# Routing inside the attention, and a second block at its end: a single-core attention and mixture-of-experts kernel

## The reference

```
x1  = layernorm(x + attention(x))                      # x: (8, 1024, 256)
gates = softmax(x1 @ gate_w);  topw, topi = top_k(gates, 2);  topw /= sum(topw)
h   = gelu(layernorm(x1 @ w1[e] + b1[e]) * ln1_g[e] + ln1_b[e])   # 256 -> 512
y_e = h @ w2[e] + b2[e]                                           # 512 -> 256
out = layernorm(layernorm(x1 + sum_k topw_k * y_topi_k) * ln_g + ln_b + x1)
```

## Time and profile before

| | us |
|---|---|
| median of 3 runs | 2865.77 (2865.7 to 2875.63) |
| profiled execution, whole | 2861.65 |
| profiled execution, span of the core | 2859.9 |
| attention's last copy of its output ends | 1800.2 |
| attention's block ends, routing begins | 1840.3 |
| routing ends, experts begin | 2070.0 |
| experts end, combine begins | 2624.6 |

### The profile page before, as it was taken

One profiled execution on the slowest core, in us unless ns is written; L12 is line 12 of the kernel. 1 busy time (PEld: TensorE's weight loads), 2 busy tenths in 40 slices (PEclk: granted clock), 3 DMA queues, 4 the chain that ended last, 5 costly groups with the idle time before them and its releaser, 6 DMA issues. The chain is left out here.

```text
span 2859.9 us, 40717 instructions
## 1 busy us (share of the span) xinstructions
PE 2070.0 (72%) x11695; PEld 1411.8 (49%) x11696; DVE 1752.2 (61%) x4841; ACT 1329.2 (46%) x3188; POOL 1324.5 (46%) x1487
## 2 busy tenths in 40 slices
PE   2588888888888888889889889400099999996000
PEld 2444554554554554555555554200088888885000
DVE  2466575576576576576576574241067777775998
ACT  0154544554555555555555556111067777775112
POOL 1354444354354354454454352157644444443885
PEclk7698998998998998998997998655599999998555
DMA  3767667667567567567667663243022222222453
GB/s 112 107 119 127 100 104 140 97 104 143 96 105 143 96 104 145 98 104 143 98 104 143 97 103 75 47 57 46 4 64 68 68 68 68 68 68 89 145 169 110
DMA packets 189312, 282.09 MB, mean 99 GB/s; under 512 B 52236, under 2 KB 110356, under 8 KB 189100
## 3 DMA queue, kind: packets, MB, share of 16 engines
q1 hardware_dynamic: 172332, 244.79, 45.7%
q0 software_dynamic: 16768, 34.69, 4.3%
HBM read 97.53 MB, written 37.62 MB: 47 GB/s over the span
## 5 line engine op out<-in xcount | busy, mean ns | idle before, releaser
L488 ACT ACTIVATE probs<-scores_T 128x512 f32<-128x512 f32 (+3 forms) x1536 | 660.0, 492 | 426.6 <-PE scores_T L387 424.2
L650 POOL TENSOR_SCALAR_AFFINE_SELECT probs<-probs 128x256 f32<-128x256 f32 x512 | 205.2, 409 | 855.7 <-ACT probs L488 854.9
L445 PE MATMUL ring<-k_stack,q_stack_b 96*128 96x512 f32 (+3 forms) x1024 | 408.0, 445 | 43.5 <-DVE neg_part L577 34.9
L577 DVE TENSOR_REDUCE neg_part<-ring 128x1 f32<-128x512 f32 x512 | 330.9, 680 | 104.5 <-PE ring L445 102.1
L582 DVE CUSTOM_DVE_ANT_0 ring<-ring,mask 128x384 f32<-128x384 f32 (+3 forms) x512 | 240.5, 515 | 243.5 <-PE ring L445 241.4
L387 PE MATMUL scores_T<-q_stack_b,k_stack 98*128 98x512 f32 (+3 forms) x1024 | 336.3, 408 | 34.0 <-ACT probs L488 33.3
L404 PE MATMUL o_ps<-probs,v_ones 128*17 128x512 f32 (+3 forms) x3072 | 357.0, 539 | 0.1
L445 PEld LDWEIGHTS ring<-k_stack,q_stack_b 96*128 96x128 f32 x1024 | 198.4, 205 | 264.5 <-DVE neg_part L577 94.6
L582 DVE CUSTOM_DVE_ANT_0 ring<-ring,mask,neg_part 128x384 f32<-128x384 f32 (+3 forms) x512 | 259.9, 554 | 68.7 <-PE ring L445 67.8
L993 ACT ACTIVATE g<-ht_ps,ln_b,ln_g 128x128 f32<-128x128 f32 x544 | 217.6, 450 | 135.6 <-PE ht_ps L943 135.6
L387 PEld LDWEIGHTS scores_T<-q_stack_b,k_stack 98*128 98x128 f32 x1024 | 200.7, 212 | 92.6 <-ACT probs L488 67.0
(11 more groups left out here) (176 smaller groups left out, 4497.9 us busy)
## 6 DMA issues: line engine op xcount, KB each, us to landing
u_rot<-u SPq DMA_DIRECT2D x128, 256.0 KB, 3.7
k_stack<-u_rot SPq DMA_DIRECT2D x128, 256.0 KB, 6.6
y_rows<-y_out SPq DMA_DIRECT2D x136, 128.0 KB, 2.1
lat_w<-lat_split SPq DMA_DIRECT2D x32, 512.0 KB, 8.1
q_stack_a<-u_rot SPq DMA_DIRECT2D x64, 256.0 KB, 7.6
q_stack_b<-u_rot SPq DMA_DIRECT2D x64, 256.0 KB, 10.3
k_stack<-u SPq DMA_DIRECT2D x64, 256.0 KB, 6.2
x_raw<-in_xT SPq DMA_DIRECT2D x16, 512.0 KB, 5.1
```

Of the source, the lines that this page charges most:

```text
L445: nc.tensor.matmul(out[:, 0:k1 - k0], q_stack[qb // 4][0:3 * L, row_buf(n, qb // 4), h, P * (qb % 4):P * (qb % 4) + P], k_stack[0:3 * L, n ...
L488: nc.scalar.activation(probs[:, s % 2, h, cols], sc[(t + j) % 3][:, HALF - w:HALF], ACT.Exp).then_inc(exp_done, 1)
L577: nc.vector.tensor_reduce(neg_part[:, n % 2, col], src[:], AX_X, ALU.max, negate=True).then_inc(max_taken, 1)
L650: nc.gpsimd.affine_select(both, both, [[0, 2], [1, P]], ALU.is_ge, zero, base=0, channel_multiplier=-1).then_inc(kept, 1)
```

## The change

`routing_phase` is gone. What it did is spread over three places.

**In the attention.** Each batch's logits stay in SBUF. A new kind R has 20 small DVE steps (`route_step`) that pick the two best experts of the batch's 1024 tokens; between them CNT, nine bf16 matmuls on PE into a bank of the ring, counts the tokens of each expert before each token. A running `base` per expert carries over from batch to batch. Each expert has its own region of 8320 rows in DRAM (`x_rows`), so that a token's place is known at once: SCAT, 16 indirect DMAs a batch from POOL, writes the batch's x1 rows (1 KB each) from `z` straight into the regions. RES, which overwrites `z`, now waits for the scatters of the batch before. RES and ZB move later, G a little earlier, and `z_T` has one buffer in place of two.

**A second block.** The main block holds all but the last steps of the last unit and the last batch (`is_late`). The second one runs those, after the attention's SBUF has been given back: ACT issues the loads of all 16 weight parts at once, straight into the place of the low part, and one split of a part (kind W) is placed behind each of 16 late C, NX and G steps. After the late steps DVE computes how many tiles each expert has and from which row each tile starts, and moves the slot numbers from regions to tiles; POOL scatters the last batch's rows and eight tiles of zero rows for padding.

**Experts and combine.** SP loads each tile as 128 rows in one piece from `x_rows` at a row number read from SBUF, in place of POOL's gather; POOL keeps the power only. In the combine PE forms `f` in PSUM from the identity times x1 and two diagonal matrices times the expert rows, and x1 plus bias from the identity and a matrix with one row of ones, all in f32: 20 matmuls of 256 columns a group. ACT makes the diagonals, eight activations a group. POOL only gathers.

```diff
-    "Y": (38, 0), "X": (-60.75, 2), "V": (-24.75, 1.125), "RES": (1.5, 0), "ZB": (9.5, 0), "C": (37.75, 1),
-    "NORM": (45.75, 0), "NX": (52.25, 0.75), "ZT": (53.5, 1.125), "G": (55, 1.125), "STORE": (68.5, 0)}
+    "Y": (38, 0), "X": (-60.75, 2), "V": (-24.75, 1.125), "RES": (18, 0), "ZB": (23.5, 0), "C": (37.75, 1),
+    "NORM": (45.75, 0), "NX": (52.25, 0.75), "ZT": (53.5, 1.125), "G": (54.375, 1.125), "STORE": (68.5, 0),
+    "R": (64.75, 0.375), "CNT": (70, 0), "SCAT": (73.5, 1)}
...
+        def is_late(it):
+            return (it[0] in ("PACK", "RCP", "INV", "Y") and it[1] == UNITS - 1
+                    or it[0] in ("C", "NORM", "NX", "ZT", "G", "STORE", "R", "CNT", "SCAT") and it[1] == B - 1)
...
                 elif kind == "RES":
                     if n:
                         sp.wait_ge(x1_stored, 16 * n)
-                        sp.wait_ge(logits_ready, TB * n)
+                        sp.wait_ge(x1_scattered, 16 * 2 * TB * n)
...
+                elif kind == "CNT":
+                    pe.wait_ge(routed, R_STEPS * n + R_CHOSEN)
+                    nc.tensor.matmul(out[:, 0:E * (TB + 1)], before[:], flat(chosen[:]), start=True, stop=False)
+                    for tb in range(TB):
...
-                    if TB * n + tb >= 2:
-                        act.wait_ge(logits_ready, TB * n + tb - 1)
-                    nc.scalar.activation(z_T[:, tb % 2, :], src[:, 0:C], ACT.Identity).then_inc(z_T_ready, 1)
+                    if TB * n + tb:
+                        act.wait_ge(logits_ready, TB * n + tb)
+                    nc.scalar.activation(z_T[:], src[:, 0:C], ACT.Identity).then_inc(z_T_ready, 1)
+                elif kind == "W":
+                    act.wait_ge(w_loaded[n], 16)
+                    w, e = parts[n]
+                    nc.scalar.activation(experts[w + "_hi"][:, e, :], experts[w + "_lo"][:, e, :].bitcast(F32),
+                                         ACT.Identity).then_inc(w_hi_ready, 1)
...
+                elif kind == "SCAT":
+                    k, tb = it[2:]
+                    if k == 0 and tb == 0:
+                        pool.wait_ge(routed, R_STEPS * n + R_STEPS)
+                        pool.wait_ge(x1_ready, TB * n + TB)
+                    j = TB * n + tb
+                    nc.gpsimd.indirect_dma_start(
+                        x_rows, bass.IndirectOffsetOnAxis(routes["slot"][:, k, j:j + 1], 0),
+                        z[:, tb, :], None).then_inc(x1_scattered, 16)
...
+        beside = [it for it in late if it[0] == "C" and it[2] >= 4 or it[0] in ("NX", "G")][:len(parts)]
+        late = [x for it in late for x in ((it, ("W", beside.index(it))) if it in beside else (it,))]
...
+            @block.scalar
+            def _(act):
+                for i, (w, e) in enumerate(parts):
+                    act.dma_start(experts[w + "_lo"][:, e, :].bitcast(F32), dram[w][:, e, :]).then_inc(w_loaded[i], 16)
+                scalar_items(act, late)
...
+            @block.gpsimd
+            def _(pool):
+                nc.gpsimd.memset(zero_rows[:], 0.0).then_inc(zero_set, 1)
+                gpsimd_items(pool, late, None)
+                for e in range(E):
+                    nc.gpsimd.indirect_dma_start(x_rows, bass.IndirectOffsetOnAxis(pad[:, e:e + 1], 0),
+                                                 zero_rows[:], None).then_inc(padded, 16)
...
+            for k in range(-5, MAX_TILES):
+                if tile(k + 5):
+                    j = k + 5
+                    row = sp.value_load(routes["row"][0:1, j:j + 1], min_val=0, max_val=ROWS - P)
+                    if j >= 4:
+                        sp.wait_ge(xt_full, j - 3)
+                    sp.dma_start(x_in[j % 4], x_rows[bass.ds(row, P), :]).then_inc(x_in_loaded[j % 4], 16)
+                if tile(k):
+                    sp.wait_ge(y_ready, k + 1)
+                    sp.dma_start(y_rows[P * k:P * k + P, :], y_out[k % 2]).then_inc(y_stored[k % 2], 16)
...
+        @block.tensor
+        def _(pe):
+            for n in range(n_groups):
+                pe.wait_ge(diag_ready, 2 * CG * (n + 1))
+                pe.wait_ge(y_loaded[n % 3], 16 * 2 * CG * (n // 3 + 1))
...
+                for t in range(CG):
+                    nc.tensor.matmul(f(n, t), routes["ident"][:], x1[n % 3][:, t, :], start=True, stop=False)
+                    for k in range(2):
+                        last = nc.tensor.matmul(f(n, t), diag[n % 2][:, t, k, :], y[k][n % 3][:, t, :],
+                                                start=False, stop=k == 1)
+                    last.then_inc(mixed, 1)
...
+                    pe.wait_ge(v_done, CG * n)
+                for t in range(CG):
+                    nc.tensor.matmul(xb(t), routes["ident"][:], x1[n % 3][:, t, :], start=True, stop=False)
+                    nc.tensor.matmul(xb(t), row0[:], b_rep[:], start=False, stop=True).then_inc(xb_ready, 1)
```

More of the change, by code:

```diff
@@ L27 @@
 HALF_TILES = MAX_TILES // 2
+CAP = B * T + P
+ROWS = E * CAP + E * P
 CG = 4
@@ new lines, in attention_phase @@
+        b_raw, b_hi, b_lo = sb("b_raw", [E, H + C]), sb("b_hi", [E, H + C], F32R), sb("b_lo", [E, H + C], F32R)
+        zero_rows, pad_f, pad = sb("zero_rows", [P, C]), sb("pad_f", [P, E]), sb("pad", [P, E], I32)
+        over, tiles, ends = sb("over", [P, E, TILES]), sb("tiles", [P, E]), [sb(f"ends{k}", [P, E]) for k in range(2)]
+        delta, count = sb("delta", [P, E]), sb("count", [P, E])
+        past, expert_f, row_f = sb("past", [P, MAX_TILES, E]), sb("expert_f", [P, MAX_TILES]), sb("row_f", [P, MAX_TILES])
@@ L675, in routing_phase, with expert_phase @@
+def expert_phase(nc, experts, routes, tail, x_rows, y_rows):
     with ExitStack() as ctx:
@@ L688, in routing_phase @@
-        pick = [sb(f"pick{k}", full) for k in range(2)]
-        rest = sb("rest", full)
-        tmp = sb("route_tmp", full)
-        tmp1 = sb("route_tmp1", [P, TILES])
-        chosen = sb("chosen", full, BF16)
-        run = [sb(f"run{k}", full) for k in range(2)]
-        pos = sb("pos", full)
-        over = sb("over", [P, E, TILES])
-        tiles = [sb(f"tiles{k}", [P, E]) for k in range(2)]
-        base = sb("base", [P, E])
-        past = sb("past", [P, MAX_TILES, E])
-        expert_f = sb("expert_f", [P, MAX_TILES])
@@ L873, in expert_phase @@
-def expert_phase(nc, experts, routes, x1_rows, y_rows):
-    with ExitStack() as ctx:
-        sb = lambda name, shape, dt=F32: ctx.enter_context(nc.sbuf_tensor(name, shape, dt))
-        sem = lambda name: ctx.enter_context(nc.semaphore(name))
-        x_in = [sb(f"x_in{a}", [P, C]) for a in range(4)]
+        x_in = [tail["z"][:, a, :] for a in range(4)]
         x_hi = [sb(f"xe_hi{a}", [P, KC, P], F32R) for a in range(2)]
@@ L890, in expert_phase @@
         g_lo = [sb(f"g_lo{a}", [P, FC, P], F32R) for a in range(2)]
-        y_out = [sb(f"y_out{a}", [P, C]) for a in range(2)]
+        y_out = [tail["z"][:, 4 + a, :] for a in range(2)]
         ps = lambda name: [ctx.enter_context(nc.psum_tensor(f"{name}{a}", [P, HALF], F32)) for a in range(2)]
```

606 lines of the change are left out of this document (317 added, 289 removed).

## The result

The changed kernel takes 2840.77 us (median of 4 executions, 2836.94 to 2843.43) where the kernel before takes 2868.44 beside it: a ratio of 0.9899, 95% interval 0.9875 to 0.9922, so about 1% faster. I had forecast 2717 and a range of 2650 to 2795. The profiled execution took 2836.94 us, its span is 2835.2.

What follows compares the result with a forecast made beforehand. PE was taken to bound attention and experts, DVE the old combine, POOL the new. 2861.65 - 155 (second block) + 42 + 8 (attention) + 0 (experts) - 42 (combine) = 2714.7, stated as 2717; range 2650 to 2795.

Steps and rivals of the forecast that it cites:

- a share of 1.2 us a batch: Attention: RES's wait on SP, routing steps, single-buffered z_T and more DMA traffic together cost 1.2 us a batch, 8 in all.
- My 42 for the scatters on POOL: Attention: scatters delay selects and k's rotation on POOL, so PE waits 7 us in each of six batches, 42 us.
- My 8 for RES's wait, the routing steps, z_T and traffic: Attention: these cost 1.2 us a batch, 8 us in all, bounds 0 and 35.
- Rival (a): Attention: scatters stand fully in PE's way, 99 + 35 us in place of 50, total 2801; chance 0.15.
- Rival (d): Attention: scatters issued against DVE's lock at 3.14 + 0.30 us each, 210 us for 42, total 2885; chance 0.03.
- 114.6: Second block: from the attention's end to the experts' start 114.6 us, 155 us less than before, bounds 135 and 170.
- 4 us for the weights: Second block, PACK to reciprocals: 4 us more as 8.4 MB of weights share the DMA engines and DVE clears the bias tile.
- the 8 us for DVE in POOL's way: Second block: DVE's table steps hold up POOL's 24 indirect DMAs, adding 8 us to their 31.7.
- rival (e): Experts: each tile waits about 2 us for rows because SP stands in a store's wait, 272 us, total 2989; chance 0.01.
- 1.26: Combine: time per gather in us for the lower bound, 52 us less; the forecast itself took 1.32, 10.6 a group.
- rival (c): Combine: PE stays at the lower clock, 17.1 us a group, +72 us in place of -42, total 2831; chance 0.07.
- cases at or below 2801: Whole kernel: forecast and neighbourhood 0.60, scatters fully in PE's way (2801) 0.15, scatters costing almost nothing (2667) 0.12.

Runs made afterwards that it cites:

- e1: The changed kernel with the residual load RES at place 25 for 18 and ZB at 31 for 23.5: 2746.88 us, ratio 0.9579.
- e8: The changed kernel with RES and ZB late and scatters behind both rotations, batch 6's at their old place: 2736.65 us, ratio 0.9538.
- e11: e8 with the attention's buffers u, q_stack, k_stack and others starting at 0 modulo 256 bytes, not 224: 2700.35 us, ratio 0.9409.
- e3: The kernel before with only RES moved from place 1.5 to 18 and ZB from 9.5 to 23.5: 2913.24 us, attention's end 47.1 us later.
- e6: The changed kernel without the scatters of batches 0 to 6 and with RES at 25, ZB at 31 (output differs): attention ends at 1857.0.
- e16: e11 unedited, run once more on one chip beside e17: 2769.85 us, ratio 0.9665.
- e17: e11 with ACT's 16 weight loads in the second block held until the last inv_rep has landed: 2757.19 us, ratio 0.9625.
- e9: The changed kernel whose combine gathers only first-choice rows, 64 gathers for 128 (output differs): combine 160.9 us.

## Why the prediction was wrong, point by point

**The attention: wrong, and the one step that missed the range.** The changed kernel, e1, e8, e11 and the kernel before, in this order, split the 173.3 us:

- 94.7 (1973.5 to 1878.8): RES's place. I wrote "RES waiting for the scatters on SP ahead of k's packing", knew the queue, and gave it a share of 1.2 us a batch. It was 94.7: 10 to 13 us in each of the six units with scatters and rotations, 7.0 in unit 2, 5.9 in unit 30. What failed is the step from the wait to its price: I did not set the time of the last scatter (place 88.5) against the time when the packs are ready (90.25, RES at 90), although the diff's own numbers say that all three fall within two places, and I did not cost the megabyte ahead of the packs although PE waits 97.5 us for those packs in the kernel before already. e3 shows that this load alone is 47 us.
- 17.0 (to 1861.8): scatters of batches 0 to 5 between the rotations and ahead of them. All 112 scatters cost 21.8 with RES late (e1 and e6).
- 30.8 (to 1831.0): the buffers' start address, nowhere in my working. It is 18 to 24 us on the changed kernel, 31 on e8, 69 on the kernel before.
- 30.8 (to 1800.2): what no edit of mine took back. Scatters where POOL has room, routing steps, one buffer for z_T, tables and the buffers at 128 are candidates; none was separated.

Each end is that of one execution. The changed attention ended at 1968.0, 1969.2 and 1973.5 in three; e11's at 1831.0, and at 1860.6 in e16, with the pauses. So the two terms of 30.8 rest on e8 and e11, run on one chip and both without the pause.

My 42 for the scatters on POOL stands against 17.0 to 21.8: the chain that I described, POOL's rotation late, ACT behind it, PE behind ACT, is in the rows (7.58 and 6.64), but I priced it at twice its worth. My 8 for RES's wait, the routing steps, z_T and traffic stands against 94.7 and what part of the last 30.8 is theirs. That 42 + 8 comes near 17.0 + 30.8 is luck. Rival (a), 134 us, was the nearest in size and wrong in kind: its scatters "fully in PE's way" cost 21.8. Rival (d), the lock at 3.44 us a scatter, did not appear: scatters in the attention take 1.00 on average (112.3 us for 112), with 0.2 ahead of each. The range left 2840 out because its upper end came from POOL's arithmetic only; no bound was made from SP's queue.

**The second block: 124.1 for 114.6, the sum nearly right by two errors.** The change of block took 7.9 us (1973.5 to 1981.4), not 1.0: the 0.96 of the earlier trace rows is DVE's wait there, not the time to the first instructions of the new block. Nothing runs and no byte moves in these 7.9 us, and why they are so long is open. SP's eight loads, 3.9 for 3.8. From PACK to the product 28.8 for 15.3: I had 4 us for the weights and they cost 17 (e17 against e16). C with its moments to NORM's end 16.9 (2016.5 to 2033.4) for 17.8; NX, ZT and G 23.6 for 24.7; routing 5.8 for 6. The 24 indirect DMAs and what follows took 34.8 for 43.7: the 8 us for DVE in POOL's way did not come, the table steps ran beside issues of 0.96 to 1.40 us. Beside nine DVE steps of 0.7 to 1.3 us no scatter was held for a whole step. The four issues over 1.00 us (1.10, 1.40, 1.07, 1.03) all overlap one of the five steps that read two SBUF tensors, and are 0.8 us longer together than at 0.96 each. The Trainium skill, SBUF — State Buffer, section SBUF: two separate sides, states the lock of the shared ports for DVE instructions in a two-port mode, and for those with two SBUF inputs only against a GpSimd instruction that reads SBUF; my forecast had left these conditions out. The trace agrees with some effect of the second kind, and not with one of a whole instruction for each step.

**The experts: right.** 555 for 554; rival (e) fell.

**The combine: right in its bound, 12 us too high.** POOL is the bound, shown by e9; the group is 10.0 and not 10.6, since the gathers' issue fell from 1038 to 946 ns when xb left POOL and f left DVE (which of the two counts was not separated; 1.26 was what I had kept for the lower end). Fifteen groups are 150 us, so the start and the end took 32 for 34.5. PE held 0.94 of its clock, so rival (c) fell: of its two levels TensorE had the higher one in nearly the whole stage (granted clock 0.79 over 2653 to 2693, 1.00 over the 100 us behind), where a product, two entries in the trace, takes 0.43 as I had:

```profile
2690.85 0.59 PE L1200 MATMUL xb_ps<-x,ident 128*128 128x256 f32 x2
2691.28 0.59 PE L1201 MATMUL xb_ps<-ln_b_rep,row 128*128 128x256 f32 x2
```

Only its first three tiles, after a wait of 15 us, ran at the lower one.

**The chances.** Faster by over 0.5% was right at 0.95, though by 1.0% and not 5.3%. I had put 0.87 on cases at or below 2801.

## What to carry to other kernels

When a step moves within an in-order queue, list what stands behind it with the time each is ready, and put its wait's end and its bytes ahead of the most urgent of them: a load of 1 MB directly ahead of the packs that TensorE waits for cost 47 us by its bytes and about as much again by its wait, and moving it back took two numbers. When buffers are allocated ahead of others, look at what their sizes do to the start addresses of everything behind, and compare the DMA queue's busy time per megabyte before and after. Before a difference of a few per cent between two runs on different chips is put down to an edit, run the unedited kernel again beside it.

## What the runs showed of the hardware that I had not expected

- SBUF-to-SBUF packs whose buffers start 32 or 224 bytes past a multiple of 256 take 97.6 and 99.0 us of a DMA engine per MB where those at a multiple take 92.5, and with no instruction changed the kernel takes 75 and 58 us longer than the one before beside it.
- Small transfers queued on one engine's ring beside 8.4 MB of loads issued by another: the sums landed 16 us after their issue (1985.3 to 2001.4), without those loads within 4.3 (1887.4 to 1891.7).
- The change from the attention's block to the second one takes 7.9 us from the last instruction to the first (7.91 to 7.92 in seven runs); the change from the experts to the combine takes 2.2 (2650.6 to 2652.8).
- One program can take 2700 us on one chip and 2770 on another, with TensorE pausing up to 2.2 us ahead of single matmuls and a loop settling from 10.0 into 11.8 us a round, while the kernel before takes 2871 and 2865.
